# q and k of a patch spectrum as 32 real and 32 imaginary parts on the same partitions, in a two-stage fp32 image kernel on Trainium2

## The reference

```python
hidden = einsum('oc,bchw->bohw', w_hidden, gn(x))      # 192 channels
hidden = depthwise_conv3x3(hidden, w_dw)
q, k, v = split(hidden, 3, axis=1)                     # 64 channels each
out = irfft2(rfft2(patches8x8(q)) * rfft2(patches8x8(k)))
out_norm = (out - mean_c) / sqrt(var_c + 1e-5) * norm_w + norm_b
x = x + einsum('oc,bchw->bohw', w_out, v * out_norm)
```

## Time and profile before

| | us |
|---|---|
| median of 3 runs | 2588.41 (2576.62 to 2591.29) |
| the profiled execution | 2588.67 |
| its span in the trace | 2586.9 |
| PE busy | 2465.4 (95%) |
| DVE busy | 1638.6 (63%) |
| ACT busy | 1432.4 (55%) |

### The profile page before, as it was taken

How to read it: one execution, slowest core, us unless ns; L and a number is a source line. 1 busy time by engine, 2 the same in 40 slices (tenths; PEclk the granted TensorE clock), 3 DMA queues, 4 the chain that set the end, 5 groups by cost and what they waited for, 6 DMA issues and landing times.

```text
span 2586.9 us, 90657 instructions
## 1 busy us (share of the span) xinstructions
PE 2465.4 (95%) x40199; PEld 1644.8 (64%) x40199; DVE 1638.6 (63%) x4058; ACT 1432.4 (55%) x2381; POOL 476.5 (18%) x324
## 2 busy tenths in 40 slices
PE   6888988969999999999999999999999999999998
PEld 3333333357777777777777777777777777777775
DVE  3566766536666666666666666666666666666665
ACT  3455656555555555555555555555555555555552
POOL 1000000002222222222222222222222222222222
PEclk9888889879999999999999999999999999999999
DMA  7588898762222222222222222222222222233222
GB/s 139 147 210 214 219 237 215 195 155 69 68 69 69 69 69 68 69 69 69 69 68 69 69 69 69 68 69 69 69 69 68 69 69 68 71 74 74 72 52 50
DMA packets 60345, 248.30 MB, mean 96 GB/s; under 512 B 12393, under 2 KB 12658, under 8 KB 53714
## 3 DMA queue, kind: packets, MB, share of 16 engines
q1 hardware_dynamic: 59954, 242.50, 38.5%
HBM read 140.74 MB, written 101.72 MB: 94 GB/s over the span
## 4 chain that ended last, share of the span: by engine, by line
PE 76%; issue 1%; ACT 1%; DVE 0%; SPq 0%; DMA 0%; ACTq 0%
PE bank L575 21%; PE bank L652 18%; PE bank L668 10%; PE bank L558 9%; PE bank L635 8%; PE bank L588 6%; PE bank L597 4%; ACT arena L821 1%; SPq L318 0%; DMA xn_d<-arena 0%; DVE arena L1110 0%; DVE arena L961 0%; ACT arena L866 0%; DVE arena L1198 0%; DVE arena L1135 0%
## 5 line engine op out<-in xcount | busy, mean ns | idle before, releaser
L441 POOL TENSOR_TENSOR arena<-arena 128x8 f32<-128x8 f32 x256 | 452.2, 1766 | 1585.1 <-DVE arena L1116 1580.1
L575 PE MATMUL bank<-arena 128*64 128x512 f16 x4608 | 689.3, 393 | 0.0
L812 ACT ACTIVATE arena<-bank 100x512 f32<-100x512 f32 x1024 | 604.2, 628 | 95.8 <-PE bank L558 74.4
L1198 DVE TENSOR_TENSOR arena<-bank,arena 128x512 f32<-128x512 f32 x512 | 352.8, 691 | 432.3 <-PE bank L652 352.4
L652 PE MATMUL bank<-arena 100*64 100x128 f32 x8192 | 511.6, 274 | 13.7 <-issue 7.0
L652 PEld LDWEIGHTS bank<-arena 100*64 100x64 f32 x8192 | 455.9, 136 | 52.6 <-issue 45.6
L558 PEld LDWEIGHTS bank<-arena 128*36 128x36 f16 (+1 forms) x8192 | 327.8, 104 | 228.0 <-ACT arena L812 12.7
L512 PE MATMUL bank<-arena 32*32 32x508 f32 (+1 forms) x9216 | 391.7, 665 | 52.6 <-issue 37.7
L558 PE MATMUL bank<-arena 128*36 128x128 f16 (+1 forms) x8192 | 388.9, 220 | 11.0 <-DVE arena L1100 4.2
L858 ACT ACTIVATE arena<-bank 128x512 f32<-128x512 f32 x256 | 149.3, 598 | 343.8 <-PE bank L635 261.7
L821 ACT ACTIVATE arena<-bank,arena 128x256 f32<-128x256 f32 x512 | 261.0, 560 | 128.5 <-PE bank L588 127.9
(11 more groups left out here) (112 smaller groups left out, 1624.1 us busy)
## 6 DMA issues: line engine op xcount, KB each, us to landing
arena<-xn_d SPq DMA_DIRECT2D x128, 536.2 KB, 8.2
xn_d<-arena SPq DMA_DIRECT2D x130, 260.0 KB, 4.5
x_d<-arena SPq DMA_DIRECT2D x64, 512.0 KB, 8.3
arena<-x_d SPq DMA_DIRECT2D x128, 256.0 KB, 4.9
out<-arena SPq DMA_DIRECT2D x128, 256.0 KB, 5.4
arena<-x_in SPq DMA_DIRECT2D x32, 544.0 KB, 10.1
arena<-x_in SPq DMA_DIRECT2D x32, 528.0 KB, 10.0
arena<-spectra_in SPq DMA_DIRECT2D x1, 1152.0 KB
```

Of the source, the lines that this page charges most:

```text
L441: pool.tensor_tensor(tiny["rstd"][:, slot], tiny["var_eps"][:, slot], powers, ALU.pow).then_inc(s_root, 1)
L575: mm = pe.matmul(v_banks[chunk % 3][64 * s:64 * s + 64, :], v_w[:, 64 * tap:64 * tap + 64], at(xs[half], row * WP + 32 * k + dx, [32 * WP, ...
L812: act.activation(h_rows[0:WIN, :, first:first + 4], banks[g % ring][0:WIN, :].rearrange("p (i c) -> p c i", i=4), ACT.Copy).then_inc(s_h_r ...
L1198: dve.tensor_tensor(parts(prod[m % 3][:, 512 * second:512 * second + 512]), parts(k_banks[n % 3]), q_sb[m % 2][:, 256 * second:256 * secon ...
```

## The change

The 64 numbers of a spectrum are now laid out as part 0 (30 real parts of pairs and 2 real frequencies) and part 1 (30 imaginary parts and the 2 other real frequencies), 32 each. q and k take the same form, G_k shrinks from 128 to 64 columns a channel, and part 0 and part 1 of a channel stand on the same 32 partitions in different columns. Four channels lie side by side. The product takes all four combinations of parts (the same 512 columns for each instruction, over four channels rather than two pairs), and the inverse sums four 32-row weights for each channel rather than two 64-row ones. In the diff below, `k_octet(m)` is left out: it is `q_octet(m)` with G_k, the second half of hwin and `k_banks[m % 2]`, and waits for products 16 u + 2 m - 2. Where `high` and the groups of windows (`some`) stand is ACT's order at the end of slot 15 and in front(0); the last piece is DVE's.

```diff
-        v_banks = [banks[3], banks[5], banks[7]]
-        k_banks = [banks[2], banks[3], banks[4]]
-        i_banks = [banks[5], banks[7]]
+        ring_banks = [banks[1], banks[3], banks[7]]
+        v_banks = [banks[2], banks[5], banks[0]]
+        q_bank = banks[0]
+        k_banks = [banks[1], banks[2]]
+        i_banks = [banks[3], banks[5], banks[7], banks[4]]
...
         hwin = take(128 * 128)
+        q_sb = [take(512) for _ in range(2)]
+        prod = take(4 * 1024)
+        assert top[0] <= first_image_free
         Y = take(64 * 64)
-        q_sb = [take(512) for _ in range(2)]
-        prod = [take(1024) for _ in range(3)]
...
         G_q = take(64 * 64)
-        G_k = take(64 * 128)
+        G_k = take(64 * 64)
...
+                if b == NB + 1:
+                    load_xs(0, 1)
                 if older is not None:
                     sp.wait_ge(s_xl_ready, 4 * (older + 1))
                     store_xn(older)
...
             sp.wait_ge(s_xn_out, 128 * NB)
-            load_xs(0, 1)
             load_res(0, 0)
...
-                for m in range(24 * step // 18, 24 * (step + 1) // 18):
+                for m in range(16 * step // 18, 16 * (step + 1) // 18):
...
                 def q_octet(m):
-                    if positive(8 * u + m - 1):
-                        pe.wait_ge(s_q_copied, 8 * u + m - 1)
-                    for pair in range(4):
-                        for par in range(2):
-                            ch = 8 * m + 2 * pair + par
-                            mm = pe.matmul(banks[m % 2][64 * par:64 * par + 64, 128 * pair:128 * pair + 128],
-                                           G_q[0:WIN, 64 * ch:64 * ch + 64], hwin[0:WIN, 128 * ch:128 * ch + 128], start=True, stop=True)
+                    if positive(8 * u + m):
+                        pe.wait_ge(s_q_copied, 8 * u + m)
+                    for quad in range(2):
+                        for part in range(2):
+                            for c in range(4):
+                                ch, first = 8 * m + 4 * quad + c, 256 * quad + 128 * part
+                                mm = pe.matmul(q_bank[32 * c:32 * c + 32, first:first + 128],
+                                               G_q[0:WIN, 64 * ch + 32 * part:64 * ch + 32 * part + 32],
+                                               hwin[0:WIN, 128 * ch:128 * ch + 128], start=True, stop=True)
                     mm.then_inc(s_q_mm, 1)
...
+                def inverse(e):
+                    pe.wait_ge(s_prod_ready, 16 * u + 4 * e + 4)
+                    if positive(16 * u + 4 * e):
+                        pe.wait_ge(s_y_ready, 16 * u + 4 * e)
...
+                    for both in range(4):
+                        for c in range(4):
                             for lam in range(2):
-                                mm = pe.matmul(i_banks[par][64 * lam:64 * lam + 64, 256 * (m % 2):256 * (m % 2) + 256],
-                                               small["inverse"][64 * par:64 * par + 64, 64 * part:64 * part + 64],
-                                               at(prod[m % 3][64 * par:64 * par + 64, :], 256 * part + 64 * lam, [512, 2], [128, 2], [1, 64]),
-                                               start=part == 0, stop=part == 1)
+                                mm = pe.matmul(i_banks[c][64 * lam:64 * lam + 64, 256 * (e % 2):256 * (e % 2) + 256],
+                                               small["inverse"][32 * c:32 * c + 32, 64 * both:64 * both + 64],
+                                               at(prod[32 * c:32 * c + 32, :], 2048 * (e % 2) + 128 * both + 64 * lam, [512, 4], [1, 64]),
+                                               start=both == 0, stop=both == 3)
                     mm.then_inc(s_inverse_mm, 1)
...
                 for m in range(8):
+                    k_octet(m)
                     if m < 7:
                         q_octet(m + 1)
...
+                    if m in (2, 4):
+                        inverse(m // 2 - 1)
+                inverse(2)
+                inverse(3)
                 v_chunk(u, half, 0, 0, 0, None)
...
+            high(NB - 2, 0)
+            high(NB - 2, 1)
...
                 if tail is None:
-                    some(8)
-                    high(NB - 2, 0)
-                    high(NB - 2, 1)
-                    some(8)
+                    some(16)
                     norm(NB - 1, 0)
                     norm(NB - 1, 1)
-                    some(16)
+                    some(8)
                     high(NB - 1, 0)
+                    some(8)
                     high(NB - 1, 1)
-                    act.wait_ge(s_xl_ready, 4 * NB)
+                    act.wait_ge(s_xl_ready, 4 * (NB - 1))
...
             def inverse_out(u, e):
+                if u == 0 and e == 0:
+                    act.wait_ge(s_xl_ready, 4 * NB)
+                act.wait_ge(s_inverse_mm, 4 * u + e + 1)
+                for c in range(4):
+                    act.activation(Y_out[:, 16 * e + c:16 * e + 16:4, :, :],
+                                   i_banks[c][:, 256 * (e % 2):256 * (e % 2) + 256].rearrange("p (c s j) -> p c s j", s=2, j=32),
+                                   ACT.Copy).then_inc(s_y_ready, 1)
...
+            for i in range(4):
+                low(NB - 2, i)
...
             front(0, 0, None)
-            dve.wait_ge(s_xn_out, 128 * NB)
             spectral(0, None, (1, 1, 0))
```

More of the change, by code:

```diff
@@ L40, in constants @@
     out["eye"] = np.tile(np.eye(32, dtype=np.float32), (4, 1))
[L42 to L54, removed]
+    u, v = np.divmod(np.arange(64), 8)
+    mirror = 8 * (-u % 8) + -v % 8
+    real = np.flatnonzero(mirror == np.arange(64))
+    pairs = np.flatnonzero(mirror > np.arange(64))
+    freq = np.concatenate([pairs, real[:2], pairs, real[2:]])
+    sine = (np.arange(64) >= 32) & (np.arange(64) < 32 + len(pairs))
+    angle = 2 * np.pi * ((u[freq][:, None] * u + v[freq][:, None] * v) % 8) / 8
+    wave = np.where(sine[:, None], np.sin(angle), np.cos(angle)).reshape(64, 8, 8)
+    spectra = np.zeros((9, 64, 10, 10), np.float64)
+    for tap in range(9):
+        dy, dx = tap // 3, tap % 3
+        spectra[tap, :, dy:dy + 8, dx:dx + 8] = wave
+    spectra = np.pad(spectra.reshape(9, 8, 8, 100), ((0, 0), (0, 0), (0, 0), (0, 28)))
+    out["spectra"] = np.pad(spectra.transpose(2, 0, 1, 3).reshape(72, 8 * 128), ((0, 24), (0, 0))).astype(np.float32)
     row, tap = np.divmod(np.arange(72), 9)
@@ L57, in constants @@
     out["row_mask"] = np.pad(np.repeat(row[:, None] == np.arange(8), 64, axis=1), ((0, 24), (0, 0))).astype(np.float32)
-    a = 2 * np.pi * ((u[:, None] * u[None, :] + v[:, None] * v[None, :]) % 8) / 8
-    both = np.concatenate([np.cos(a) + np.sin(a), np.sin(a) - np.cos(a)], axis=1) / 64
-    out["inverse"] = np.tile(both, (2, 1)).astype(np.float32)
+    cosines, sines = np.cos(angle), np.sin(angle)
+    paired = np.arange(32)[:, None] < len(pairs)
+    inverse = np.concatenate([np.where(paired, 2, 1) * cosines[:32], np.where(paired, 2 * sines[:32], 0), np.where(paired, 2 * sines[:32], 0),
+                              np.where(paired, -2, 1) * cosines[32:]], axis=1) / 64
+    out["inverse"] = np.tile(inverse, (4, 1)).astype(np.float32)
     return out
@@ L240, in build @@
         xq = [take(BAND * W) for _ in range(3)]
-        x2_1, x2_2, x2_0 = [take(QPIX) for _ in range(3)]
+        x2_1, x2_2 = [take(QPIX) for _ in range(2)]
+        conv_w = [take(9 * 32) for _ in range(2)]
+        first_image_free = top[0]
+        x2_0 = take(QPIX)
         x2 = [x2_0, x2_1, x2_2]
@@ L557, in hidden_group @@
                     for low, high in ((0, 64), (64, WIN)):
-                        mm = pe.matmul(banks[g % ring][low:high, 128 * i:128 * i + 128], w[:, first + low:first + high], hidden_w,
+                        mm = pe.matmul(ring[g % len(ring)][low:high, 128 * i:128 * i + 128], w[:, first + low:first + high], hidden_w,
                                        start=True, stop=True)
@@ L637, in q_octet, with k_octet @@
                     mm.then_inc(s_q_mm, 1)
[L639 to L642, removed]
+                def k_octet(m):
+                    if positive(16 * u + 2 * m - 2):
+                        pe.wait_ge(s_prod_ready, 16 * u + 2 * m - 2)
+                    if m == 1 and tail is not None:
                         pe.wait_ge(s_gated, 8 * u - 1)
-                    if n == 2 and tail is not None:
-                        pe.wait_ge(s_t_copied, 8 * u)
-                    for pair in range(2):
+                    for quad in range(2):
@@ L647, in k_quad @@
                         for part in range(2):
-                            if octet is not None and pair == 1 and part == 1:
-                                inverse_inputs(octet)
-                            for par in range(2):
-                                ch = 4 * n + 2 * pair + par
-                                mm = pe.matmul(k_banks[n % 3][64 * par:64 * par + 64, 256 * part + 128 * pair:256 * part + 128 * pair + 128],
```

(13 more changed lines are left out.)

118 lines of the change are left out of this document (47 added, 71 removed).

## The result

| | before | after |
|---|---|---|
| median, same chip | 2584.86 us (2576.62 to 2591.29) | 2650.23 us (2635.95 to 2657.54) |
| ratio, 95% interval | | 1.0248 (1.0194 to 1.0302) |
| profiled execution | 2588.67 | 2649.98 |
| PE busy | 2465.4 | 2332.2 |
| mean granted clock of PE | 0.972 | 0.945 |

The forecast was 2406 us, in a range of 2365 to 2490. The kernel became 2.5% slower, so the forecast has the wrong sign and misses by 244 us. The page of the kernel after, to be set against the earlier trace rows: busy time by engine, then one DMA queue (packets, MB, share of the 16 DMA engines), then the chain's shares.

What follows compares the result with a forecast made beforehand. PE, busy 95% of the span, was taken to bound the kernel: 2588.67 less 170 (units), 8 (change of stages) and 5 (start) gives 2405.7, said as 2406 us, range 2365 to 2490.

Steps and rivals of the forecast that it cites:

- stage 2 goes at PE's pace and a change is worth what it takes from PE's line or adds to it as a wait: Opening step on the whole of stage 2: PE, busy 95% of the span and 76% of the chain, sets the time.
- Units: 32 x (5.4 - 0.1) = 170 us: Stage 2's 32 units: each spectral part saves 5.4 us, each front pays 0.1, together 170 us less.
- the items that are paid once: Savings outside the repeated units: 8 us at the change of stages and 5 us at the start.
- Octets of q and k, 0.89 on four tiles: Spectral part: 32 records of 128 columns take 0.89 us; 15 octets take 13.4 us instead of 20.1.
- Inverse, 2.0 on eight tiles: Spectral part: each of four inverses, 64 records of 256 columns, takes 2.0 us; 8.0 a unit instead of 7.93.
- Evictions of 256 columns and the stall, 1.22 and 1.35: Between the last two inverses: ACT's four evictions take 1.22 us, and PE's resulting wait is counted as 1.35 us.
- octet 7's products are ready under the third inverse: End of the spectral part: two products, 1.35 us, start when the k octet ends and finish within the inverse's 2.0 us.
- A spectral part, 24.1: Sum of one unit's q, k, inverses, projection, shape changes and stall: 24.1 us against 29.48, 5.4 less.
- The cover of q's copy: Between q octets: the one-bank copy wait of 0.79 us is hidden by the k octet of 0.89, 0.1 us to spare.
- The front, 0.1 paid: Front of each unit: the last eviction ends 1.22 instead of 1.09 us after its start, charged as 0.1 us.
- Change of stages and start, 8 and 5: Once each: DVE's DMA wait before its first product goes, 8 us (4 to 10.3); smaller transform table, 5 us (0 to 9).
- Rival 3: q and k octets: four weights of the same 100 rows do not run together, octets 1.75 us, total 2819 us; chance 5%.

Runs made afterwards that it cites:

- e1: The changed kernel with stage 2's window-row loads, x2 loads and output stores cut to a sixteenth of their bytes from unit 1 on: 2385.52 us, 0.9218 of the kernel before.
- e5: The changed kernel with window rows loaded in eight pieces and the four output stores, each paced by q or k octets, same bytes: 2432.17 us, 0.9384 of before.
- e2: The kernel before with the same cut of stage-2 transfers to a sixteenth as e1, as its control: 2568.29 us, 0.9932 of the kernel before.
- e4: The changed kernel with the third inverse moved behind q octet 7, ahead of k octet 7: 2651.10 us, 1.0228 of the kernel before.

## Why the prediction was wrong

**The step that failed** is the first one, "stage 2 goes at PE's pace and a change is worth what it takes from PE's line or adds to it as a wait". Behind it stands the sum "Units: 32 x (5.4 - 0.1) = 170 us", which counts what an instruction takes to run, and the waits on semaphores, and nothing for bringing the instructions in. That term was left at nothing without a reason, and it measured 265 us. No rival priced it either. The mean unit, from first q octet to first q octet over the 30 units behind the first, is 63.1 us before, 66.2 after, 57.5 in e1 and 58.8 in e5: after differs from e1 by 8.7 us, and 30 x 8.7 = 261. That is more than the whole miss of 244: e1 lies 20 us under the forecast. Without the bursts the change is worth 2568.3 - 2385.5 = 183 us, and 183 was forecast. That the two are equal is in part luck. The unit of e2 is 62.7 us, so the change brings 5.1 a unit, 164 us, where 170 were counted, while the items that are paid once brought more than their 13.

The change doubled the rate at which q and k use up instructions, and that was to be read ahead of the result. The change's own order listing shows 16 matmuls for 8 in a q octet. The page of before has the instruction queue, 317 packets of 16 KB. And its convolution, the one stretch of short records under a DMA share of 0.9, already had the symptom, a line that was read past (waits of the kernel before):

```profile
PE bank L512 <- issue: 37.7, 21, 4.6
```

Those stops carry the same mark: in the kernel before, 20 stops of stage 1, 37.5 us, fall on the same place in a block of 256 and end 1.2 to 1.8 us after a packet of q8. So PE waits for instructions there too. Every run here has them, and none changed stage 1's transfers, so that they would go with its bursts is not shown.

The Trainium skill (Runtime: NRT & Kernel Launch, "Instruction fetch mechanics") says that an engine's instruction memory is refilled in blocks of 256 instructions over a DMA queue of its own, and that this is mostly hidden because instructions are dispatched more slowly than fetched. The trace agrees with the block (255.5 records for each added packet) and with the queue, and not with the last part: in the kernel after, the fetch is hidden only while no burst of data is queued, and it cost 265 us of 2650.

**Step by step.**

- *Octets of q and k, 0.89 on four tiles:* right. 0.87 to 0.90 at full clock, double the rate of two tiles. Loads of the same 100 rows lie beside running matmuls here too: in 1110.00 to 1118.90 PEld is busy for 6.36 us and PE for 8.71.
- *Inverse, 2.0 on eight tiles:* right. 1.93 to 2.02.
- *Evictions of 256 columns and the stall, 1.22 and 1.35:* right, 1.22 and 1.46. The argument beside it, that octet 7's products are ready under the third inverse, holds only while that inverse stands there (e4).
- *A spectral part, 24.1:* right where no burst falls. In e1 it runs from 1001.11 to 1025.18, 24.07. The cover of q's copy held: no wait of PE for L857 stands among PE's waits in e1. In the kernel after each unit has at least one stop: they take 64 to 71 us where those of e1 take 57.5 to 57.8.
- *The front, 0.1 paid:* not seen. From the inverse's end to the turn is 6.04 us in e1 (1025.18 to 1031.22), as it was the earlier trace rows.
- *Change of stages and start, 8 and 5:* too small. The first convolution record starts at 41.64 instead of 51.63, the first q octet of stage 2 at 526.8 instead of 545.7, and DVE's first product at 530.88 instead of 564.03. e1 against e2 gives 18 us to the first q octet and 10 more in unit 0 beyond a unit's usual gain: some 29 instead of 13, though these starts differ by 8 us between profiles of kernels with the same stage 1 (526.8 and 534.6).
- *Rival 3 (slower)* had the sign right and the mechanism wrong: octets never ran at 1.75 for want of tiles. They do take 1.94 behind a stop, at 1.2 GHz, which at a glance looks alike; the window's clock tells them apart.

**Still open.** In e5 a unit is 1.2 us longer than in e1, and small issue stops are left. Whether a v chunk between the last two inverses would cover the wait of 1.46 was not tried. The loss of 265 us is accounted for by the stops (159) and the estimate for the lower clock (77 to 102); the last 4 to 29 us are in no row. Why a packet of q8 starts late is shown only as far as the timing goes: one packet in ten of the kernel after starts over 6.5 us behind the earliest place, in e1 over 1.7, and none takes much longer once started. The trace does not tell on which of the 16 engines it waited.

## What to carry to other kernels

When a change makes matmuls shorter or more numerous, work out how long one packet of instructions (here some 128 loads and matmuls) now lasts, and compare it with the longest burst of data that can be queued ahead of a fetch; if the packet runs out first, the gain turns into "issue" stops and a lower clock. Splitting the same transfers and tying each piece to the progress of the engine that must be fed costs nothing: it turned 2650 us into 2432. A row of "issue" waits in a stretch of short instructions and busy DMA is the sign to look for before making another stretch like it. If the stops all fall on one place of a 256-instruction block, each just behind an instruction packet, it is this one.

## What the runs showed of the hardware

- Instruction packets of 16 KB for PE start late while a burst of data is queued: none in 8.1 us in which the 16 DMA engines were full (102.6% by the view), one right after. Once started, a packet takes 0.9 to 1.5 us, with bursts (after) or without (e1).
- PE ran dry at one and the same place in a block of 256 instructions, in 60 of 60 stops of the kernel after's stage 2, some 300 instructions behind the earliest start of the missing packet.
- Stops of 3 to 5 us with no matmul take the granted clock from 1.00 to near 0.5 for the next few us (0.56 over 5.72 us, octets in 1.94 instead of 0.87), so a stop of 5.33 us cost about half as much again.
- Matmuls on four column tiles that hold the same 100 rows ran at double the rate of two tiles: 32 records of 128 columns in 0.87 us, where two tiles did 16 in 0.873.
- Four plain evictions of 256 columns on ACT take 1.22 us where two of 512 take 1.09.
